# ScalarE scales the MLP's input rows two batches ahead, VectorE's added steps move ahead of the output wait, and the experts' first transpose joins the MLP's last round

## What is computed

```python
# third layer, after the state-space scan (x is here its sum, Y in the kernel)
h = rmsnorm(x, scale2)
h = jax.nn.gelu(h @ w1 + b1, approximate=False) @ w2 + b2
return x + h
...
x = x + _layernorm(_L1_attn_ref(_layernorm(x, axis=-1), ...), axis=-1)
x = x + _layernorm(_L1_ffn_ref(_layernorm(x, axis=-1), ...), axis=-1)   # experts
# experts, first steps
spikes_enc = jax.nn.sigmoid(inputs_embeds @ enc_W + enc_b)
cont = flat @ s2c_W + s2c_b
logits = jnp.tanh(cont @ rW1 + rb1) @ rW2 + rb2
```

## Time and profile before

| what | us |
|---|---|
| median of 3 runs | 1330.01 |
| lowest and highest | 1327.49, 1330.76 |
| profiled execution, its own time | 1335.36 |
| span of its trace | 1333.6 |
| mean granted TensorE clock | 0.965 of full speed |

### The profile page before, as it was taken

The page is one execution under the profiler, slowest core; times in us unless marked ns, Lnnn a source line. Parts: engine busy times, 40 slices in busy tenths (PEclk is TensorE's granted clock), DMA queues, the critical chain, the costliest instruction groups (busy, mean ns, idle before and its releaser), DMA issues. The chain is left out here.

```text
span 1333.6 us, 27407 instructions
## 1 busy us (share of the span) xinstructions
PE 1185.9 (89%) x7410; PEld 529.1 (40%) x7410; DVE 954.6 (72%) x3025; ACT 909.3 (68%) x1352; POOL 652.2 (49%) x1101
## 2 busy tenths in 40 slices
PE   4989999999999999996999468999979999999995
PEld 2222222222222222223666367766633434434342
DVE  5677777777777776775788775566555788888764
ACT  3878999999999999995666580333424666666654
POOL 5425555555555556532555441233133556656544
PEclk9989999999999999998999789999959999999998
DMA  5663555555555655504940021000000000000001
GB/s 156 137 120 90 98 105 105 109 109 103 105 104 102 114 107 107 107 6 123 238 129 0 1 68 60 0 1 0 0 1 0 9 10 16 8 16 16 9 17 32
DMA packets 71700, 87.97 MB, mean 66 GB/s; under 512 B 10368, under 2 KB 65190, under 8 KB 66022
## 3 DMA queue, kind: packets, MB, share of 16 engines
q1 hardware_dynamic: 69326, 85.81, 30.4%
q10 hardware_dynamic: 2296, 1.25, 0.4%
HBM read 63.84 MB, written 31.59 MB: 72 GB/s over the span
## 5 line engine op out<-in xcount | busy, mean ns | idle before, releaser
L562 ACT ACTIVATE a_probs<-a_S 128x1024 f32<-128x1024 f32 x512 | 496.7, 1037 | 53.9 <-DVE a_S L708 46.7
L708 DVE TENSOR_TENSOR a_S<-a_S,a_tables 128x256 f32<-128x256 f32 (+1 forms) x512 | 281.3, 561 | 148.7 <-PE a_S L578 145.8
L585 PE MATMUL a_O<-a_probs,a_V 128*32 128x512 f32 x2048 | 276.2, 612 | 2.4 <-ACT a_probs L562 0.6
L578 PE MATMUL a_S<-a_Qs,a_Ks 48*128 48x512 bf16 x1024 | 180.5, 389 | 15.1 <-ACT a_probs L562 11.0
L578 PEld LDWEIGHTS a_S<-a_Qs,a_Ks 48*128 48x128 bf16 x1024 | 42.7, 93 | 231.8 <-ACT a_probs L562 196.6
L2248 ACT ACTIVATE e_hid<-e_H 128x512 f32<-128x512 f32 x128 | 69.5, 595 | 59.2 <-PE e_H L2366 59.2
L1958 ACT ACTIVATE g_hid<-g_H,w_b 128x512 f32<-128x512 f32 x64 | 44.0, 687 | 91.1 <-PE g_H L1985 91.1
L455 POOL CAST a_parts<-a_whole 128x512 bf16<-128x512 f32 x45 | 27.4, 610 | 153.7 <-DVE a_whole L718 153.7
L2364 PE MATMUL e_H<-e_gated,w_We 64*128 64x512 f32 x256 | 73.2, 648 | 1.3 <-ACT e_hid L2248 1.2
L585 PEld LDWEIGHTS a_O<-a_probs,a_V 128*32 128x32 f32 x2048 | 40.5, 108 | 82.6 <-issue 67.4
L2375 PE MATMUL e_O<-e_hid,w_We 128*64 128x512 f32 x256 | 68.7, 609 | 0.4 <-ACT e_hid L2248 0.4
(11 more groups left out here) (402 smaller groups left out, 2397.9 us busy)
## 6 DMA issues: line engine op xcount, KB each, us to landing
a_parts_dram<-a_parts SPq DMA_DIRECT2D x94, 192.0 KB, 5.5
a_Qs<-a_parts_dram SPq DMA_DIRECT2D x60, 192.0 KB
m_taps_by_step<-h_taps SPq DMA_DIRECT2D x8, 1024.0 KB, 13.2
m_taps<-m_taps_by_step SPq DMA_DIRECT2D x8, 1024.0 KB, 5.1
a_Qs<-a_parts_dram SPq DMA_DIRECT2D x60, 128.0 KB
a_Ks<-a_parts_dram SPq DMA_DIRECT2D x30, 192.0 KB
a_Qs<-a_parts_dram SPq DMA_DIRECT2D x68, 64.0 KB
XY<-L_attn_x SPq DMA_DIRECT2D x16, 256.0 KB, 7.2
```

Of the source, the lines that this page charges most:

```text
L562: act.activation(probs[n % KEPT][:], S[n % RING][:], ACT.Exp).then_inc(exped, 1)
L578: mm = pe.matmul(S[n % RING][:, par, :], Ks[p][rows, pr, kb * P:(kb + 1) * P], Qs[p][Q_OF(kb)][rows, pr, :], start=True, stop=True)
L585: mm = pe.matmul(O[VC * j:VC * (j + 1), :], V[q][:, kb, HG * g + j, :], probs[(2 * m + j // 2) % KEPT][:, j % 2, :], start=(kb == 0), stop ...
L708: v.tensor_tensor(s[:, :, where], s[:, :, where], wide, ALU.mult).then_inc(corrected, 1)
```

## The change

Three things are done together.

1. ScalarE makes yn instead of VectorE. Behind the gelus of round t it scales batch t + 2, as soon as the transposes of batch t + 1 have read yn; batch 1 is scaled ahead of the rounds, and batch 0 still by VectorE. So that the reciprocal roots are there, squares and inversion run three batches ahead (AHEAD = 3) in place of two.
2. VectorE's added step of rounds 4 to 12 (`step_ahead`) stands ahead of the wait for OUT in the same round, not behind the statistics. In the last round `settle_later` goes ahead of that wait too, and the wait for the last add to end is gone.
3. In round 14 VectorE normalises x of batch 0 for the experts into the MLP's yn (`next_layer_norm`). In the last round TensorE's four transposes, which were idle work, transpose it, and VectorE copies it to a new buffer first_xT. The experts' TensorE begins with the product by encW from first_xT; the normalisation, transpose and copy at the experts' start are gone, GpSimd no longer waits for them, and TensorE's wait for two constants (`init`) comes behind these products.

```diff
-        joins_by = lambda u: turn_of_join(u) + 1 + 2 * u
+        joins_by = lambda u: turn_of_join(u) + 2 * u
+        AHEAD = 3
+        comes = lambda t, ahead: not isinstance(t, int) or t + ahead < B
...
+            def rms_norm(b):
+                act.wait_ge(power.inverted, b * Norm.INVERT + Norm.INVERT)
+                TP.read(act, yT_use(b - 1))
+                for c in range(NT):
+                    op = act.activation(yn[:, c], Y[:, b + 1, c], ACT.Identity, scale=rstd[:, b, c:c + 1])
+                op.then_inc(yn_done, 1)
+
             def body(t, p, i):
                 for m in range(FC):
                     act.wait_ge(h_full, t * FC + (m + 1))
                     act.activation(hid[p][:, m], H[m][:], ACT.Gelu, bias=b1[:, m:m + 1]).then_inc(h_free, 1)
-
-            in_pairs(act, B, body)
+                if comes(t, 2):
+                    rms_norm(t + 2)
...
+            def next_layer_norm():
+                v.wait_ge(ahead.inverted, (of_sum(0) + 1) * Norm.INVERT)
+                TP.read(v, yT_use(B - 1))
+                for c in range(NT):
+                    op = v.tensor_scalar(yn[:, c], X[:, 0, c], core.xmean[:, 0, c:c + 1], core.xrstd[:, 0, c:c + 1],
+                                         ALU.subtract, ALU.mult)
                 op.then_inc(yn_done, 1)
...
-            def body(t, p, i, last=False):
-                rms_norm(t + 1) if not last else v.tensor_copy(yn[:], Y[:, 0]).then_inc(yn_done, 1)
-                take_T(t + 1, 1 - p)
-                if not isinstance(t, int) or t + 2 < B:
-                    power.squares_of(v, t + 2, Y[:, t + 3])
+            power.squares_of(v, 2, Y[:, 3])
+
+            def body(t, p, i):
+                last = isinstance(t, int) and t == B - 1
+                if last:
+                    take_transposed(v.tensor_copy, v, TP, yT_use(B), core.first_xT[:])
+                else:
+                    take_T(t + 1, 1 - p)
+                if comes(t, AHEAD):
+                    power.squares_of(v, t + AHEAD, Y[:, t + (AHEAD + 1)])
+                if isinstance(t, int) and t == B - 2:
+                    next_layer_norm()
+                if isinstance(t, int):
+                    step_ahead(t)
                 if last:
                     measure_later()
+                    settle_later()
                 OUT[p].read(v, i + 1)
                 y = Y[:, t + 1].rearrange("p c d -> p (c d)")
                 OUT[p].emptied(v.tensor_tensor(y, y, OUT[p].t[:], ALU.add))
-                OUT[p].after(v, i + 1)
                 if last:
                     return
+                OUT[p].after(v, i + 1)
...
-            pool.wait_ge(TP.full, FIRST_XT)
-            pool.sem_inc(core.turns, 1)
+            pool.sem_inc(xn_done, 1)
             layer_norm(1)
...
-            take_xT(FIRST_XT)
...
-            pe.wait_ge(init, 2)
-
...
-            x_T(0, FIRST_XT)
+            skip(TP, FIRST_XT)
             for m in range(HC):
-                encoder(FIRST_XT, 1, m)
+                encoder(FIRST_XT, 1, m, core.first_xT)
+            pe.wait_ge(init, 2)
             rounds(pe, body)
```

More of the change, by code:

```diff
@@ L1931, in _ @@
             power.constant(pool, init, 0)
[L1932 to L1940, removed]
+            for b in range(AHEAD):
+                power.invert(pool, b, rstd)
+            with pool.Fori(0, LOOPED) as t:
+                power.invert(pool, t + AHEAD, rstd)
             for t in range(LOOPED, B):
-                if t + 2 < B:
-                    power.invert(pool, t + 2, rstd)
+                if comes(t, AHEAD):
+                    power.invert(pool, t + AHEAD, rstd)
                 for u in range(FIRST):
@@ L1958, in body @@
                     act.activation(hid[p][:, m], H[m][:], ACT.Gelu, bias=b1[:, m:m + 1]).then_inc(h_free, 1)
-            in_pairs(act, B, body)
+                if comes(t, 2):
+                    rms_norm(t + 2)
+            rms_norm(1)
+            with act.Fori(0, B // 2 - 1) as i:
+                for p in range(2):
+                    body(i * 2 + p, p, i)
+            for t in (B - 2, B - 1):
+                body(t, t % 2, t // 2)
             act.preload_act_table(ACT.Sqrt)
@@ L2002, in _, with rms_norm_first @@
         def _(v):
-            def rms_norm(b, last=False):
-                v.wait_ge(power.inverted, b * Norm.INVERT + Norm.INVERT)
+            def rms_norm_first():
+                v.wait_ge(power.inverted, Norm.INVERT)
                 for c in range(NT):
-                    op = v.tensor_scalar(yn[:, c], Y[:, b + 1, c], rstd[:, b, c:c + 1], None, ALU.mult)
+                    op = v.tensor_scalar(yn[:, c], Y[:, 1, c], rstd[:, 0, c:c + 1], None, ALU.mult)
+                op.then_inc(yn_done, 1)
+            def next_layer_norm():
[4 more added lines that the diff above has]
+                                         ALU.subtract, ALU.mult)
                 op.then_inc(yn_done, 1)
@@ L2017, in _ @@
             W.take_folded(v, folding)
-            rms_norm(0)
+            rms_norm_first()
             take_T(0, 0)
-            def body(t, p, i, last=False):
-                rms_norm(t + 1) if not last else v.tensor_copy(yn[:], Y[:, 0]).then_inc(yn_done, 1)
-                take_T(t + 1, 1 - p)
-                if not isinstance(t, int) or t + 2 < B:
-                    power.squares_of(v, t + 2, Y[:, t + 3])
+            power.squares_of(v, 2, Y[:, 3])
[5 more added lines that the diff above has]
+                    take_T(t + 1, 1 - p)
+                if comes(t, AHEAD):
+                    power.squares_of(v, t + AHEAD, Y[:, t + (AHEAD + 1)])
[3 more added lines that the diff above has]
+                    step_ahead(t)
                 if last:
                     measure_later()
+                    settle_later()
                 OUT[p].read(v, i + 1)
@@ L2046, in join, with step_ahead @@
                 v.tensor_tensor(X[:, u], X[:, u], Y[:, u + 1], ALU.add).then_inc(measured, 1)
+            def step_ahead(t):
+                for u in range(FIRST):
+                    if t == turn_of_output(u):
+                        ahead.moments_of(v, of_output(u), Y[:, u + 1], p=of_output(u))
+                    if t == turn_of_join(u):
+                        join(u)
+                    if t == turn_of_sum(u):
+                        v.wait_ge(measured, joins_by(u) + 2)
+                        ahead.moments_of(v, of_sum(u), X[:, u], core.xmean, p=of_sum(u), to=u)
             tick = Tally(v, measured, start=BULK)
@@ L2320, in x_T, with encoder @@
                 transposed(core, pe, TP, n, xn)
-            def encoder(n_xT, n, m):
+            def encoder(n_xT, n, m, src=xnT):
                 TP.after(pe, n_xT)
                 EB[m].fill(pe, n)
-                EB[m].filled(pe.matmul(EB[m].t[:], W.encW[:, tile_of(core, m)], xnT[:], start=True, stop=True))
+                EB[m].filled(pe.matmul(EB[m].t[:], W.encW[:, tile_of(core, m)], src[:], start=True, stop=True))
             def cells(i):
@@ L2561, in body @@
                     OB.emptied(v.tensor_copy(moeT[:], OB.t[:]))
[L2563 to L2566, removed]
             joined.moments_of(v, LAST, Y[:, B])
@@ L2593, in program @@
             state_space(core, I, W, flt, taps)
+        core.first_xT = ctx.enter_context(nc.sbuf_tensor("first_xT", [D, core.T], F32))
         mlp(core, I, W)
```

## The result

| | median us | lowest to highest | executions |
|---|---|---|---|
| before | 1330.38 | 1325.72 to 1335.64 | 8 |
| changed | 1320.13 | 1316.34 to 1324.06 | 8 |

The ratio is 0.9922 with a 95% interval of 0.9904 to 0.994: 10.4 us faster, between 8.0 and 12.8. The forecast was 1319.1, the range 1313.0 to 1322.8.

What follows compares the result with a forecast made beforehand. TensorE was taken to wait in MLP rounds for yn, late behind VectorE's added step, and at the experts' start. Rounds -8.0, boundary -2.4 and clock -0.5 make -10.9 us off the median 1330.01: 1319.1, range 1313.0 to 1322.8.

Steps and rivals of the forecast that it cites:

- The rounds, -8.0 us: MLP rounds: TensorE's wait for yn goes, nine rounds fall from 76.98 us to 7.66 each, -8.0 us.
- ScalarE's cost and the room behind it: MLP rounds: four scalings take 1.64 us of ScalarE's 4.39 us free; GpSimd's root has 2.3 us of room.
- The slower rival, table loads: MLP rounds: scaling needs another function table, two loads a round on ScalarE, time 1336.6 or 1355 us; chance 0.03.
- The boundary, -2.4 us: Between MLP and experts: the first product by encW begins at 968.0 in place of 970.38, -2.4 us, bounds -3.2 to -0.7.
- the 1.4 us for TensorE's way into the block: Experts' start: TensorE's first product comes 1.4 us after VectorE's first instruction, with some 17 semaphore instructions ahead.
- the row at hand: MLP's start: TensorE's first weight load comes 0.57 us after VectorE's first instruction, five semaphore instructions ahead; used for the estimate.
- settle_later's share: MLP's end: two small instructions go ahead of the last add, so VectorE's next block starts 0.73 us earlier.
- The clock, -0.5 us: Experts' start: with 2.4 us idle in place of 3.4, TensorE's clock falls a product or so later, -0.5 us.
- at most -12, where other engines will hold much of it back: Clock term's bound: full clock through the stretch to 1000.3 saves half of 23.77 busy us, at most -12.
- The rival in which the clock holds: Experts' start: full clock lasts through the first products or longer, 1315.9 us, down to some 1312; chance 0.2.
- The spread: Whole kernel: the range's upper end, 1322.8 us, allows a run-to-run spread of under 1 us.
- The boundary gives nothing: Experts' start: the way into the block is long, only the rounds' gain is left, 1322.0 us; chance 0.1.

Runs made afterwards that it cites:

- e1: Kernel before with only VectorE's added steps of rounds 4 to 12 moved ahead of the wait for OUT; median 1323.31 us, ratio 0.9947.
- e2: Kernel before with only yn made by ScalarE, two batches ahead, added steps and experts' start as before; median 1323.75 us, ratio 0.9947.
- e3: Changed kernel with the experts' start undone, both parts in the rounds and settle_later's move kept; median 1323.19 us, ratio 0.9949.
- e9: The changed kernel run again, same program, against the kernel before; median 1319.5 us, ratio 0.9905.
- e6: Changed kernel with the experts' first products ahead of everything in TensorE's queue, plus idle matmuls in its gaps; median 1313.46 us, ratio 0.9876.

## Why the prediction was right

- **The rounds, -8.0 us:** right in the trace, and e1, e2 and e3 bear it out. The rounds are TensorE's own 7.66 us, as the undisturbed ones before had shown. What the prediction did not say is that its change has two cures for one wait in it: yn leaving VectorE, and the step moving into the idle 1.57 us. It wrote the first as the cause of the gain and the second as its neighbour. Each alone gives all of it.
- **ScalarE's cost and the room behind it:** 1.64 us put, 1.28 measured. ScalarE waited for GpSimd's root once, ahead of the rounds (6.1 us), and in the rounds neither the root nor the transposes held it. The slower rival, table loads, did not come.
- **The boundary, -2.4 us:** -1.88 in the trace. The step that was too small is the 1.4 us for TensorE's way into the block, which took 1.87: 0.07 us a semaphore instruction was put, 0.11 is measured. The 0.57 us of the row at hand, shared among its own five semaphore instructions and not among eight steps, would have given 0.11. settle_later's share was put at 0.73 and is 0.78.
- **The clock, -0.5 us:** its mean effect can't be told from zero: -8.0 and -1.9 make -9.9 of the measured -10.4. Its size in one execution was taken too small, and its reason, that the shorter idle time would matter, has no support in e1, e3 and e9. By the end of the range, "at most -12, where other engines will hold much of it back", 9.5 us lie between the profile of before, at 0.52, and that of e6, at full clock, which differ by more than the clock; between two executions of the changed kernel it is 7.8. The rival in which the clock holds, 1315.9, is what the profiled execution, 1316.34, looks like; the median does not. The rule cited there (the Trainium skill, "TensorE: Matmul & The Clock Gate", Part 1), that a program changes clock at different places from run to run, is what three profiles of the changed kernel show: 0.89, 0.73 and 0.56.
- **The spread:** "under 1 us" was wrong for single executions, which lie 7.7 us apart. The forecast of the profiled span, 1322.7, missed the measured 1314.3 by 8.4 us, most of it behind the first product and 1.4 ahead of the MLP. The median came out within 1.0 us of the forecast, partly by chance: the boundary's shortfall of 0.5 and the clock's uncertainty are of that size or more.
- **The boundary gives nothing:** e1 has the rounds' gain alone, with a median of 1323.31. The changed kernel's medians are below it in all three sets, and its trace shows the 1.88 us.

## What to carry to other kernels

When an engine in a ring waits for a small step, look first where in its queue the producer idles: moving the added step into that idle time gave all of the gain, and moving the work to another engine gave the same and no more. Count the semaphore instructions ahead of an engine's first work in a block, and put work that needs none of them first. Where a stretch with gaps follows a busy one, compare several executions before a few us are put down to an edit: two executions of the changed kernel differed by 7.8 us behind the boundary, with a granted clock of 0.89 and 0.56 in the first 31 of them. Idle matmuls in the gaps gave 2.3 ± 1.3 us back against the kernel beside them, where they stood in nobody's way.

## What the runs showed of the hardware

- Behind the same gap of 2.93 us before the same work the clock stayed full for one execution's first product (1.95 us) and was half in another's (3.75 us). In the kernel before it was half for 29.9 us; in e6, with idle matmuls in the gaps, it was full in all of the 31 us.
- The semaphore instructions ahead of TensorE's first work in a block took 0.11 us each on average (17 of them, 1.87 us), those that open a bank 0.15.
- One of ScalarE's instructions on a 128x128 tile took 0.39 us with a scale for each partition and no shift, and 0.48 with both the earlier trace rows; in a row they overlap, and come to 0.32 (1.28 for four) and 0.41 (22.9 us for 56) each. The Trainium skill ("ScalarE: Activation LUTs", What ACT_TABLE_LOAD costs) says that each such operand adds about 93 ns; the rows agree, with 0.09.
